# Five gathered heads and three dense heads in a memory-layer tower: 8-column weights, score pieces stacked by DMA, a new order of work

## The reference, cut to what matters

```python
# 32 batches, each on its own: waveform (1, 10240) -> h (128, 64)
h = tokenizer(x)                       # 4 strided convolutions, norms, a small MLP, soft pooling
h = h + linear_attention(layernorm(h)) # the "mixer": 6 projections, triangular solve, norm, gate
# memory layer, 8 heads, causal attention over 128 positions of a batch (2 x 256 rows in the task's shapes)
sim = einsum(queries, pk_keys)                   # two lists of 64 key scores per head and token
scores, idx = top_k(sim, 16)                     # top 16 of each list
score = scores[0][:, None] + scores[1][None, :]  # 256 pair sums
final, pk_idx = top_k(score, 16)                 # the best 16 pairs -> 16 of 4096 table rows
w = softmax(final)
k = einsum(w, keys_table[ind]); v = einsum(w, values_table[ind])
out = softmax(causal(q k)) v ; h = h + out @ Wo
```

## Time and profile before

| | us |
|---|---|
| median of 3 runs (4036.1 to 4037.41) | 4037.06 |
| profiled execution, span | 4037.6 |
| PE busy | 3556.1 (88%) |
| POOL busy | 2942.1 (73%) |
| DVE busy | 2916.6 (72%) |
| ACT busy | 2746.8 (68%) |

### The profile page before, as it was taken

How to read it: one execution, slowest core, us unless ns; L and a number is a source line. 1 busy time by engine, 2 the same in 40 slices (tenths; PEclk the granted TensorE clock), 3 DMA queues, 4 the chain that set the end, 5 groups by cost and what they waited for, 6 DMA issues and landing times.

```text
span 4037.6 us, 71484 instructions
## 1 busy us (share of the span) xinstructions
PE 3556.1 (88%) x21240; PEld 2640.5 (65%) x21240; DVE 2916.6 (72%) x13918; ACT 2746.8 (68%) x7870; POOL 2942.1 (73%) x3079
## 2 busy tenths in 40 slices
PE   9789999999989888889888889888889888889677
PEld 6367666667666666667666666666667666667556
DVE  3577778887777777777777777777777777777661
ACT  4467777777767677767677767677767677767444
POOL 0477777777777777777777777777777777777776
PEclk9699999999999999999999999999999999999788
DMA  3112222222222222222222222222222222222211
GB/s 115 30 51 53 54 54 54 53 54 55 54 53 54 54 53 55 54 54 54 55 53 54 54 54 54 54 53 54 54 54 54 54 53 54 54 54 54 53 53 50
DMA packets 108453, 220.17 MB, mean 55 GB/s; under 512 B 55768, under 2 KB 56192, under 8 KB 107552
## 3 DMA queue, kind: packets, MB, share of 16 engines
q0 software_dynamic: 98304, 201.52, 19.0%
q1 hardware_dynamic: 9760, 14.08, 1.1%
HBM read 214.36 MB, written 1.05 MB: 53 GB/s over the span
## 4 chain that ended last, share of the span: by engine, by line
POOL 37%; PE 21%; DVE 15%; issue 15%; ACT 11%; DMA 1%; DVEq 0%; SPq 0%; POOLq 0%; ACTq 0%
POOL got L755 37%; PE bank L1062 5%; ACT diag L1307 3%; PE bank L843 2%; DVE pick L1736 2%; DVE dist L1740 2%; PE bank L1039 2%; PE bank L826 1%; ACT L1093 1%; PE bank L1017 1%; PE bank L829 1%; ACT d_exp L1286 1%; DMA got<-in_table,rows 1%; DVE d_w L1774 1%; DVE rowf L1670 1%
## 5 line engine op out<-in xcount | busy, mean ns | idle before, releaser
L755 POOL DMA_INDIRECT got<-in_table,rows x3072 | 2940.9, 957 | 1085.5 <-issue 925.3
L1307 ACT ACTIVATE diag<-cst,weight 128x128 f32<-128x128 f32 x3072 | 944.7, 393 | 1.0 <-PE bank L1062 0.4
L1062 PE MATMUL bank<-diag,got 128*128 128x128 f32 x6144 | 803.0, 294 | 17.1 <-DMA got<-in_table,rows 9.3
L1062 PEld LDWEIGHTS bank<-diag,got 128*128 128x128 f32 x6144 | 770.3, 207 | 41.5 <-issue 19.5
L1039 PE MATMUL bank<-d_w,tab 128*128 128x128 f32 x4096 | 646.3, 283 | 0.5 <-DVE d_w L1774 0.5
L1774 DVE SCALAR_TENSOR_TENSOR d_w<-bank,d_exp 128x256 f32<-128x256 f32 x1024 | 420.7, 421 | 259.8 <-ACT d_exp L1286 109.3
L1039 PEld LDWEIGHTS bank<-d_w,tab 128*128 128x128 f32 x4096 | 553.8, 196 | 13.2 <-issue 0.8
L1286 ACT ACTIVATE d_exp<-bank 128x256 f32<-128x256 f32 x1024 | 378.2, 376 | 189.8 <-PE bank L1019 188.9
L1017 PE MATMUL bank<-d_top,sel 128*128 128x512 bf16 x1024 | 400.6, 391 | 116.8 <-DVE d_w L1774 116.5
L843 PE MATMUL bank<-h,conv_w 128*128 128x512 f32 (+2 forms) x1024 | 337.7, 478 | 9.3 <-DVE h L1430 7.1
L1017 PEld LDWEIGHTS bank<-d_top,sel 128*128 128x128 bf16 x1024 | 115.5, 113 | 267.0 <-DVE d_w L1774 167.8
(11 more groups left out here) (307 smaller groups left out, 6400.6 us busy)
## 6 DMA issues: line engine op xcount, KB each, us to landing
got<-in_table,rows POOLq DMA_INDIRECT x3072, 2.5
tab<-in_table SPq DMA_DIRECT2D x2, 2048.0 KB, 16.7
got<-in_pairs SPq DMA_DIRECT2D x1, 2048.0 KB, 8.8
wave<-in_x SPq DMA_DIRECT2D x32, 50.0 KB
cst<-in_consts SPq DMA_DIRECT2D x1, 1059.0 KB, 6.9
mlp<-in_mw SPq DMA_DIRECT2D x1, 1024.0 KB, 9.4
out_h<-res_o SPq DMA_DIRECT2D x32, 32.0 KB
conv_w<-in_w SPq DMA_DIRECT2D x1, 512.0 KB, 4.0
```

The lines of the kernel that those rows point to most:

```text
L755: pool.indirect_dma_start(got[:, g, k, :], None, table, bass.IndirectOffsetOnAxis(ap=rows[:, h * TOPK + k:h * TOPK + k + 1], axis=0)).then ...
L1062: last = mm(kvt_ps, got[:, j % NGB, k, :], diag[:, j % NDG, k, :], start=k == 0, stop=k == TOPK - 1)
L1307: last = a(diag[:, (b * NG + h) % NDG, k, :], const("ident"), ACT.Copy, scale=weight[:, b % 2, h, k:k + 1])
```

## The change

- Head 5 becomes a dense head. Five heads are gathered (80 indirect DMAs a batch in place of 96), three are dense.
- A gather now brings the 16 rows of each of 8 tokens: the row numbers are turned by DVE transposes (`row_t`), so that partitions hold picks and the columns of the list hold tokens. PE multiplies each gathered tile by an 8-column weight tile (`spread_w`, built by one DVE instruction per group from transposed weights) with start and stop in one product. The diagonals and ACT's 96 instructions for them are gone. `got` has three buffers, `rows` two; DVE no longer waits for gathers.
- Dense heads: a unit is now one head and two chunks (48 units a batch). The three bf16 parts of the score are written to DRAM (`parts`) and read back by 12 DMAs per head into `stacked`, each block of 32 keys beside the others; one 128-column product with `stack_sel` adds the three parts. A unit has four bf16 products of 128 columns (two for scores, two for distances) and two f32 table products. ACT writes the exponential into `d_w`, where DVE masks it in place. The table product of unit u-1 stands ahead of the scores of unit u+1.
- The mixer's copies (`rk`, `val`, five `prod`, `rhs0`, `sol1`, `offsol`) move from DVE to ACT; four instructions of its output norm become three.
- DVE's chains wait only where a result is needed, with independent instructions between.
- Sums get a stage of their own (`group`) apart from `head`. One table of positions, in millionths of a step, for seven stages and all batches; the tables for the first and last steps are gone. SP follows the same order.

```diff
-DENSE = (6, 7)
+DENSE = (5, 6, 7)
 ND = len(DENSE)
 NG = HEADS - ND
 CHUNKS = NKEY * NKEY // P
-UNITS = CHUNKS
+BLOCK = 32
+TILES = CHUNKS // 2
+UNITS = ND * TILES
+STACK_DMAS = 12
...
-SUMS_LATE = 2
-SCORES_LATE = 5
-DENSE_LATE = 12
-NGB = 4
+NGB = 3
+SLOTS = 8
 QUARTER = 4
 PARTS = 4
-NDG = 2
...
+                    order += [(b * STEP + t, stage, k, b, name) for k, (t, name) in enumerate(zip(at, hops, strict=True))]
+            return [(b, stage, name) for _, stage, _, b, name in sorted(order)]
...
+            def dense(b):
+                yield "sw"
+                sp.wait_ge(s_d_in, b + 1)
+                sp.dma_start(parts[b % 2, :, :], d_parts[:, :, :, :].rearrange("p k i t -> p (k i t)")).then_inc(s_parts, 16)
+                for i in range(ND):
+                    yield f"s{i}"
+                    n = b * ND + i
+                    sp.wait_ge(s_parts, 16 * (b + 1))
+                    if n > 1:
+                        sp.wait_ge(s_pairs, (n - 1) * TILES)
+                    of = parts[b % 2, :, :].rearrange("p (k i t) -> k i p t", k=3, i=ND)
+                    for k in range(3):
+                        for a in range(2):
+                            to = stacked[:, n % 2, a * TILES // 2:(a + 1) * TILES // 2, :]
+                            sp.dma_start(to[k * BLOCK:(k + 1) * BLOCK, :, :],
+                                         of[k, i, a * BLOCK:(a + 1) * BLOCK, :].unsqueeze(1).broadcast_to([BLOCK, TILES // 2, P])).then_inc(s_stack[n % 2], 16)
+                            sp.dma_start(to[3 * BLOCK + 8 * k:3 * BLOCK + 8 * k + 8, :, :],
+                                         of[k, i, NKEY:, :].rearrange("(g j) t -> j g t", j=8)).then_inc(s_stack[n % 2], 16)
...
                     for k in range(TOPK):
-                        if n >= NGB and k == TOPK - QUARTER:
-                            past, at = (n - NGB) // NG, (n - NGB) % NG
-                            pool.wait_ge(s_q_ps, past * HEADS + place_of(past, at) + 1)
-                        elif n >= NGB and k % QUARTER == 0:
-                            pool.wait_ge(s_summed, (n - NGB) * (TOPK // QUARTER - 1) + k // QUARTER + 1)
-                        pool.indirect_dma_start(got[:, g, k, :], None, table,
-                                                bass.IndirectOffsetOnAxis(ap=rows[:, h * TOPK + k:h * TOPK + k + 1], axis=0)
-                                                ).then_inc(s_last[k // QUARTER] if n == BATCH * NG - 1 else s_got[g], 16)
+                        if n >= NGB and k % QUARTER == 0:
+                            pool.wait_ge(s_summed, (n - NGB) * (TOPK // QUARTER) + k // QUARTER + 1)
...
             def pair_scores(b, u):
 
-                if u > 1:
...
-                mm(scores, sel[:, u, :], d_low[:, :, :].rearrange("k i t -> k (i t)"), start=False, stop=True).then_inc(s_pairs, 1)
+                i, tile = u // TILES, u % TILES
+                n, c = b * ND + i, 2 * tile
+                if tile == 0:
+                    pe.wait_ge(s_stack[n % 2], (n // 2 + 1) * 16 * STACK_DMAS)
+                ps = pair_bank[u % 2]
+                for x in range(2):
+                    mm(ps[:, x * P:(x + 1) * P], stack_sel[:, x, :], stacked[:, n % 2, tile, :], start=x == 0, stop=False)
+                for x in range(2):
+                    last = mm(ps[:, (2 + x) * P:(3 + x) * P], sel[:, c + x, :], d_dist[:, i, :], start=False, stop=x == 1)
+                last.then_inc(s_pairs, 1)
 
             def groups(b, which):
                 for u in which:
...
             def table_sum(b, u):
                 yield f"v{u}"
+                i, tile = u // TILES, u % TILES
                 pe.wait_ge(s_d_w, b * UNITS + u + 1)
...
-                for i in range(ND):
-                    last = mm(acc_bank[:, i * P:(i + 1) * P], tab[:, i, u, :], d_w[:, u % 2, i, :],
-                              start=False, stop=u == UNITS - 1 and i == ND - 1)
-                last.then_inc(s_d_sum, 1)
+                if tile == 0 and b * ND + i:
+                    pe.wait_ge(s_kvd, b * ND + i)
+                for x in range(2):
+                    last = mm(acc_bank[:, i * P:(i + 1) * P], tab[:, i, 2 * tile + x, :], d_w[:, u % 2, x, :],
+                              start=tile == x == 0, stop=tile == TILES - 1 and x == 1)
+                if tile == TILES - 1:
+                    last.then_inc(s_d_sum, 1)
...
+            def group(b, g):
+                n = b * NG + g
+                yield f"a{g}"
...
+                    pe.wait_ge(s_added, BEFORE[5, b, g][0])
+                if n < BATCH * NG - 1:
+                    pe.wait_ge(s_got[n % NGB], (n // NGB + 1) * 16 * TOPK)
+                for k in range(TOPK):
+                    if n == BATCH * NG - 1 and k % QUARTER == 0:
+                        pe.wait_ge(s_last[k // QUARTER], 16 * QUARTER)
+                    last = mm(kvt_ps[:, k * SLOTS:(k + 1) * SLOTS], got[:, n % NGB, k, :], spread_w[:, n % NGB, k, :], start=True, stop=True)
+                    if k % QUARTER == QUARTER - 1:
+                        last.then_inc(s_summed, 1)
...
+                a(rk[:, :, :].rearrange("p a t -> p (a t)"), my[0:D, 0:2 * P], ACT.Copy).then_inc(s_mact, 1)
+                a(val[:, :], mx[:, 2 * P:2 * P + D], ACT.Copy).then_inc(s_mact, 1)
...
+                for lv in range(LEVELS - 1):
+                    yield f"pc{lv}"
+                    mpe(f"p{lv}")
+                    a(prod[:, :], my[:, 256:384], ACT.Copy).then_inc(s_mact, 1)
...
+            def group(b, g):
+                n, h = b * NG + g, g // 2 * 2
...
+                    act.wait_ge(s_score, (b - 1) * HEADS + place_of(b - 1, min(h + 1, NG - 1)) + 1)
+                if h + 1 < NG:
+                    to = kvt[:, h:h + 2, :].rearrange("p h (q f j) -> p f h q j", q=4, f=2)[:, g % 2, :, :, :]
+                    a(to, kvt_ps.rearrange("p (j q h) -> p h q j", q=4, h=2), ACT.Copy).then_inc(s_kv, 1)
+                else:
+                    a(kvt[:, h, :].rearrange("p (c j) -> p c j", c=SLOTS), kvt_ps.rearrange("p (j c) -> p c j", c=SLOTS), ACT.Copy).then_inc(s_kv, 1)
...
                     vec.wait_ge(s_d_exp, b * UNITS + u + 1)
-                    if u >= 2 or b > 0:
-                        vec.wait_ge(s_d_sum, b * UNITS + u - 1)
-                    stt(d_w[:, u % 2, :, :].rearrange("p k t -> p (k t)"), pair_bank[u % 2][:, 2 * P:4 * P], TOPK - 0.5,
...
+                    stt(both, pair_bank[u % 2][:, 2 * P:4 * P], TOPK - 0.5, both, ALU.is_lt, ALU.mult).then_inc(s_d_w, 1)
+
+            def group(b, g):
+                n = b * NG + g
+                yield f"b{g}"
+                if g == 0:
...
+                    vec.wait_ge(s_second, b * NSECOND + R2["w_t"])
+                if n >= NGB:
...
+                    vec.wait_ge(s_summed, (n - NGB + 1) * (TOPK // QUARTER))
+                full = [P, TOPK, 4, 2]
+                slots = const("group").rearrange("p (q o) -> p q o", q=4).unsqueeze(1).broadcast_to(full)
+                if g < HALF:
+                    share = weight_t[:, b % 2, g, :].unsqueeze(2).unsqueeze(3).broadcast_to(full)
+                else:
+                    share = weight_t[:, b % 2, HALF:, :].rearrange("p o j -> p j o").unsqueeze(2).broadcast_to(full)
+                tt(spread_w[:, n % NGB, :, :].rearrange("p j (q o) -> p j q o", q=4), share, slots, ALU.mult).then_inc(s_spread, 1)
```

More of the change, by code:

```diff
@@ new lines, in pipeline, with each, program @@
+        def pipeline(eng, *stages):
+            shares = {(stage, b): program(b) for stage, program in enumerate(stages) for b in range(BATCH)}
+            nxt = {of: next(g, None) for of, g in shares.items()}
+            for b, stage, name in PLAN:
+                if nxt[stage, b] == name:
+                    nxt[stage, b] = next(shares[stage, b], None)
+            assert not any(nxt.values()), nxt
+        def each(count, unit):
+            def program(b):
+                for u in range(count):
+                    yield from unit(b, u)
+            return program
@@ L1083, in head @@
                 mm(y_ps, prob_t[:, :], vw[:, :], start=True, stop=True).then_inc(s_y, 1)
[L1085 removed]
+            pipeline(pe, tokenizer, mixer, nothing, nothing, dense, each(NG, group), each(HEADS, head))
         @block.scalar
@@ L1326, in head @@
                 a(prob_t[:, :], prob_ps, ACT.Copy).then_inc(s_prob_t, 1)
-            pipeline(act, tokenizer, mixer, second, dense, in_turn(NG, SUMS_LATE, weighted, nothing, nothing),
-                     in_turn(HEADS, SCORES_LATE, head, nothing, nothing))
+            pipeline(act, tokenizer, mixer, route, second, dense, each(NG, group), each(HEADS, head))
         @block.vector
@@ L1600, in choose, with sums @@
+                inc(last)
+            def choose(first, end, gathered, inc, own, read):
                 every, found = slice(first, end), slice(first, gathered)
                 ng = gathered - first
-                yield "keys"
-                cp(top[:, 1, found, 0, :], topi[:, found, 0, :])
```

(22 more changed lines are left out.)

937 lines of the change are left out of this document (482 added, 455 removed), and 158 rows, old and new, of tables (AT, ENDS_AT).

## The result

The changed kernel takes 4871.03 us (median of 3 runs, 4867.73 to 4875.55) against 4037.06: a ratio of 1.2067, 95% interval 1.2048 to 1.2086. Its profiled run has a span of 4869.2 us at a mean granted clock of 0.77; the kernel before has 0.933.

The account below looks back on a forecast made before the run. GpSimd's gather issue rate was taken to bound the kernel before. First store 370, thirty batches at 113.5 us (3405) and a last batch of 80 summed to 3855 us; range 3660 to 4090.

Parts of the forecast that it names:

- the paragraph on PE: TensorE's work per batch: sums -3.7 us, dense units +7.8, f32 product and transposes -0.2; together +4, 97 us of stream.
- the term of 18.4 us a batch: Gathered sums on TensorE: 80 narrow products at 0.23 us from start to start, against 22.1 us a batch before.
- the list of what would make it wrong: Closing signs of failure: mask waits over 0.47 us a unit, back-to-back gathers, stack waits over 5 us, half-clock stretches behind waits.
- the waiting that I chose: TensorE's waiting per batch, taken as 16.5 us on top of 97 us of stream, giving a pace of 113.5 us.
- the third (gain stops, 118.4): Rival: gain stops at the gathers; TensorE's +4 adds to the old free pace of 114.4, 4002 us; chance 0.14.
- GpSimd: Gathers: 80 at 1.2585 us, 100.7 us a batch, no longer the bound, with waits for rows or sums beside them.
- Dense unit: TensorE's dense part: 0.30 us for four bf16 products plus 0.45 for table passes, 0.75 a unit, 36.0 a batch.
- DMA and SP: Stacking score parts through DRAM: TensorE may wait about 3 us once a batch; the pieces' DMA time is hidden by slack.
- First store: First batch's output store, put at 370 us (245 + 125), where it stood at 350 before.
- Rival 4: Slower through the dense round trip: 0.65 us of waiting a unit, pace 128, 4290 us; decides from 0.47; chance 0.18.
- rival 5: GpSimd stays the bound, gathers slowed by stack pieces or three buffers, 1.5 us each, 120 us a batch, 4040; chance 0.03.

Follow-up runs that it names:

- experiment 1: Changed kernel with each gathered product streaming all 128 columns of its head's weights, sixteen products accumulating (gathered sums wrong in value): 4215.04 us.
- experiment 7: The kernel of experiment 1 with the mask applied to 128 of a unit's 256 columns: 4189.04 us against 4215.04.
- (5): Changed kernel with weights zero-padded to 128 columns, one weight tile for three buffers, two buffers of gathered rows for three; right result: 4377.0 us.
- (6): The zero-padded kernel of (5) with the next unit's scores again ahead of the previous unit's table product, and a third exponentials buffer: 4461.24 us.
- (3): Changed kernel with product k streaming columns 8k to 128 of its head's weights, 68 on average, right result: 4480 us.

## Why the prediction was wrong

**The step that failed** stands in the paragraph on PE: "Narrow weights save ACT its diagonals, not PE its time". It prices the narrow product by its starts alone and puts its effect on the clock at nothing. At full clock the price holds: the passes of the changed kernel's sums start 0.111 us apart, those of 128 columns 0.114, so a product is 0.22 us and the term of 18.4 us a batch was 17.7. What had no term is the clock. I took every PE price at 2.4 GHz from rows of a kernel at 0.97, and moved sixteen times fewer columns without asking what the clock would do. Half-clock stretches stood only in the list of what would make it wrong, and "behind such waits"; 125 of them came behind work. At 1.2 GHz a pass of the sum takes 0.213 us, and so does everything after it until the clock is back: L762, 698 ns before under its old number L829, is 961 here. Price: 4871 - 4215 = 656 us, for 2237 - 406 = 1831 us more at 1.2 GHz.

The Trainium skill, "TensorE: Matmul & The Clock Gate", section HAM oscillation — how this bites in real kernels, has the clock fall where TensorE idles between bursts of work. Of the changed kernel's 218 falls 92 agree with that: in the 5 us ahead of each, TensorE is idle for 0.57 us or more, 2.2 us on average. The other 126 come in or just behind a sum.

**The other 360 us** (4215 - 3855) are for the most part the waiting that I chose. By the stores of experiment 1 (392.4, 4128.0, 4212.2): first store +22, thirty batches at 124.5 in place of 113.5 +330, the last batch with its end +7 (86.6 in place of 80). TensorE's busy time a batch rose from 105.8 to 0.884 x 125.2 = 110.6, by 4.8 where 4 was predicted. The idle time rose from 114.4 - 105.8 = 8.6 to 14.6 us, where I had let it shrink by 4.5. PE's waits in 16 batches of experiment 1, and in the 6 of before from 350 to 1036 us:

```profile
PE bank L972 <- DVE d_w L1782: 112.0, 159, 2.4
PE bank L1028 <- ACT prob_t L1282: 31.4, 16, 2.0
PE bank L990 <- DVE res L1816: 22.6, 32, 1.1
PE bank L873 <- ACT prod L1182: 17.8, 32, 0.8
```

```profile
PE bank L1017 <- DVE d_w L1774: 21.0, 30, 1.6
PE bank L935 <- DVE inv L1528: 12.4, 15, 1.2
```

A batch now waits 7.0 us for masks (was 3.5), 2.0 once for a head's transposed probabilities, and 1.4 for heads that must leave the bank before a sum. ScalarE and VectorE with time to spare did not shorten TensorE's waits; I read these as the waits of an in-order stream at fixed turns. By the rivals this is the third (gain stops, 118.4) plus 6 us of waiting. That TensorE's stream and these waits make up the 125.2 is arithmetic; that removing one would shorten it was not shown, and experiment 7 speaks against a simple sum.

**Point by point.** GpSimd: right, (2507.5 + 743.0) / 2560 = 1.27 us a gather with waits beside it. Dense unit: right; in experiment 1 at full clock the four bf16 products take 0.23 us, where I took 0.30 and set 0.32 beside it, and the table products 0.45 to 0.55, together near the 0.75. VectorE: 2979.8 / 32 = 93 us a batch, 98 predicted. ScalarE: 67, 65 predicted. DMA and SP: the stack costs even less than the 3 us a batch allowed for, TensorE waits 1.9 us for it in the whole run. First store: 370 predicted, 392 at full clock and 416 as it was. Rival 4 (slower, chance 0.18) had the sign and not the reason: the wait for masks was 160.4 / 1536 = 0.10 us a unit, far from its 0.47. Two slips change nothing: rival 5's sum gives 4050 and not 4040, and the eight independent instructions of the earlier trace rows start 0.13 us apart, not 0.14. The result lies 780 us outside the range, whose bounds all came from costs at one clock.

No version beat the kernel before. Those with a right result took 4377 (5), 4461 (6) and 4480 us (3); even experiment 1 is 4.5% above it (ratio 1.0448, 1.042 to 1.0475), since GpSimd's bound held the kernel before at only 121.1 us a batch, against 125.2.

## What to carry to other kernels

A product that streamed few columns saved nothing at full clock here and took the clock away from what followed, so before narrowing a TensorE operand, look at the granted clock and give "everything after it at 1.2 GHz" a price of its own. If little is to be computed, two forms kept the clock here: the small operand as the stationary one, and zeros, or columns that are overwritten, streamed beside it. None of them was timed as a gain over the kernel before. And idle time on other engines is no credit: in experiment 1 TensorE's idle time grew by 6 us a batch while VectorE stood idle for 30% of the time and ScalarE for 49%.

## What the runs showed of the hardware

- The granted clock fell although TensorE had no idle time from a sum's first pass to the fall: 125 of 126 sums of 16 products with 8 streamed columns, 92 of 114 with 32; with 128 columns it fell in 2 of 129.
- The clock rises within 128-column sums (31 of 31) and within sums with 8 stationary and 128 streamed columns (96 of 96 and 93 of 94), never within 8-column ones (0 of 34).
- f32 passes start 0.111 us apart for 8 streamed columns, 0.114 for 128, and 0.109 with 8 stationary ones: neither narrow side makes a product cheaper. At 1.2 GHz 8 columns take 0.213 us.
- Four bf16 products of 128 columns, each with its own weights, take 0.23 us from the first start to the start of what follows.
